# mLSTM values with tokens on the output's partitions, and scores and weights handled by pairs of heads

## The chip, the cores and the metric

The kernel runs on one core of one Trainium2 chip. The metric is the time of one execution on the device, in microseconds (us). Before the change three runs took 670.98, 671.68 and 671.97 us, a median of 671.68.

## What is computed

Four layers follow one another on a hidden state of 4 sequences of 256 tokens with 256 channels: attention with rotary parts, a gated feed-forward layer, an mLSTM block with its own feed-forward layer, and a feed-forward layer with int8 weights. Each ends in a layer norm of input plus output. The change lies in the mLSTM, of which this is the core (8 heads, 16 channels for queries and keys, 32 for values):

```python
Dmat = Fcum[..., :, None] - Fcum[..., None, :] + i_pre[..., None, :]
Dmat = jnp.where(causal, Dmat, -jnp.inf)
m = jnp.max(Dmat, axis=-1, keepdims=True)
Smat = jnp.exp(Dmat - m)
qk = jnp.einsum('bhsd,bhtd->bhst', q, k) / jnp.sqrt(jnp.float32(dqk))
C = qk * Smat
n = jnp.maximum(jnp.abs(jnp.sum(C, axis=-1, keepdims=True)), jnp.exp(-m))
h = jnp.einsum('bhst,bhtd->bhsd', C / n, v)
```

A root-mean-square norm per head, a sigmoid gate and the output projection follow.

## The kernel before, in words

Every engine has its own hand-written program (`@block.tensor`, `scalar`, `vector`, `gpsimd`, `sync`), and they meet by counting semaphores alone. Whatever stands behind a waiting instruction on its engine waits too. The order in each program is fixed by the loops `for c in range(B)` (4 sequences, called chunks here) and `for pair in range(PAIRS)` (4 pairs of heads), so there are 16 steps of one pair. This is the heads stage. Ahead of it stand the projections (L1482 to L1484), behind it the block's feed-forward layer (`ffn_pe` with kind 1, L1229 to L1269), into whose steps the rest of the head work of the last chunks is hooked (`finish_heads`).

One pair goes through five pieces of work before the change:

- **scores** (TensorE, L1548 and L1549): for each head, keys stand as the stationary operand (32 rows, 128 columns), queries stream: 256 columns, then 128, each in two parts of an fp32r split. A head has a PSUM bank of its own, UG0 or UG1, and may begin once the DVE has weighed the head two before it (`c_ready`).
- **decay** (ScalarE, L1720 and L1721): the exponential of the decay rows of one head, 256 and 128 columns, into one of four buffers.
- **weigh** (DVE, L1907): scores from PSUM times decay, 384 columns, for one head, into one of four weight buffers. The left 256 columns are key tile 0 against all 256 queries, the last 128 are key tile 1 against query tile 1.
- **values** (TensorE, L1563, L1565, L1567): the values `V1` of a head (128 tokens by 32 channels and a column of ones) stand as the stationary operand, 33 columns; the weights stream, 128 columns at a time. The output has channels on its partitions. The two heads of a pair use different halves of the array's columns (output partitions 0 to 32 and 64 to 96 of bank UG2 or UG3). These are fp32 matmuls, each of which is two instructions (two LDWEIGHTS and two MATMULs) in the trace.
- **take_pair** (ScalarE, L1729) copies that output into `gt`, and **back** (TensorE, L1576) transposes it, two transposes per pair, into the bank pair `OUTS`, with tokens on the partitions. After four pairs `take` (ScalarE, L1736) copies `OUTS` to `hraw`, and `squares`, `head_sums` (DVE, L1918 to L1925), `head_scales` (GpSimd, L2072 to L2083), `norm_b` (DVE, L1934, L1939), `heads_T` (TensorE, L1588), `hoT` and `project_out` (TensorE, L1482 again, output `X`) follow, some of them one or two chunks later.

TensorE also runs `keep_busy` (L1605), matmuls with no result that anybody reads: four after the first scores, one each in the steps (2, 0), (2, 1) and (3, 0) (chunk, pair). The DVE also adds the causal mask to the decay rows (`mask_rows`, L1898).

Of the kernel before, what the change touches and what calls it, by code (L numbers as in the profile page):

```python
# [21 lines left out]
P = 128  # L22
# [943 lines left out]
def layers(nc, keep, wl_d, wg_d, bg_d, cols_d, mask_d, wm_d, w8_d, sdown_d, out_d):  # L966
# [5 lines left out]
    with keep["both"], ExitStack() as ctx:  # L972
# [9 lines left out]
        def halves(a):  # L982
# [47 lines left out]

        A = [a[:, :].rearrange("p (h n) -> p h n", h=HM) for a in (stage, stage1)]

        decay_buf = [ga[:, 0, :], ga[:, 1, :], rows[:, 768:1152], rows[:, 1152:1536]]
        weight_buf = [gb[:, 0, :], gb[:, 1, :], rows[:, 0:384], rows[:, 384:768]]
        og_v = x1[:, :, :].rearrange("p (c t) d -> p c t d", c=B)
        scr_m = nc.dram_tensor("scr_m", (B, 32, S + P), F32).ap()

        UG = [pb(f"UG{i}") for i in range(4)]
        OUTS = pb("OUTS", (P, 2, 512))
        TB, X = keep["TB"], keep["X"]  # L1040

# [5 lines left out]
            st_ready e_ready c_ready pv_ready vt_ready back_ready taken abs_ready nn_ready n2_ready n2_squared sq_ready msq_ready hv_ready  # L1047
# [429 lines left out]
        def _(pe):  # L1477
# [61 lines left out]
            def scores(c, h):  # L1539

                r, n = slice(32 * (h % 4), 32 * (h % 4) + 32), (h // 4) * S
                if h == 0:
                    pe.wait_ge(s_["qk_split"], 2 * B if c == 0 else 2 * (c + 1))
                if c or h >= 2:
                    pe.wait_ge(s_["c_ready"], HM * c + h - 1)
                bank = UG[h % 2]
                for keys, q, out in ((n, slice(n, n + S), bank[:, 0:S]), (n + P, slice(n + P, n + S), bank[:, S:S + P])):
                    pe.matmul(out, stack(c, 1)[r, keys:keys + P], stack(c, 0)[r, q], start=True, stop=False)  # L1548
                    last = pe.matmul(out, stack(c, 2)[r, keys:keys + P], stack(c, 0)[r, q], start=False, stop=True)  # L1549
                last.then_inc(s_["st_ready"], 1)  # L1550

            def values(c, pair):

                two = (2 * pair, 2 * pair + 1)
                pe.wait_ge(s_["c_ready"], HM * c + 2 * pair + 2)
                if c == 0 and pair == 0:
                    pe.wait_ge(s_["og_ready"], TT * B)
                if c or pair >= 2:
                    pe.wait_ge(s_["vt_ready"], HM // 2 * c + pair - 1)
                w = [weight_buf[(HM * c + h) % 4] for h in two]  # L1560
                out = [UG[2 + pair % 2][i * 64:i * 64 + DH + 1, 0:S] for i in range(2)]
                for i, h in enumerate(two):
                    pe.matmul(out[i][:, 0:P], V1[:, c, 0, h, :], w[i][:, 0:P], start=True, stop=True)  # L1563
                for i, h in enumerate(two):
                    pe.matmul(out[i][:, P:S], V1[:, c, 0, h, :], w[i][:, P:S], start=True, stop=False)  # L1565
                for i, h in enumerate(two):
                    pe.matmul(out[i][:, P:S], V1[:, c, 1, h, :], w[i][:, S:S + P], start=False,  # L1567
                              stop=True).then_inc(s_["pv_ready"], 1)

            def back(c, pair):  # L1570

                pe.wait_ge(s_["vt_ready"], HM // 2 * c + pair + 1)
                if c and pair == 0:
                    pe.wait_ge(s_["taken"], c)
                for t in range(TT):
                    last = pe.transpose(OUTS[:, t, pair * P:pair * P + PAIR], gt[0:PAIR, pair % 2, t * P:(t + 1) * P],  # L1576
                                        ident[0:PAIR, 0:PAIR])
                last.then_inc(s_["back_ready"], 1)

            def heads_T(c):  # L1580
                pe.wait_ge(s_["ho_ready"], c + 1)
# [25 lines left out]
            def heads(c):  # L1607
                if c == 0:
                    scores(0, 0)
                    scores(0, 1)  # L1610
                    keep_busy(4)
                for pair in range(PAIRS):
                    if pair + 1 < PAIRS:
                        scores(c, 2 * pair + 2)
                        scores(c, 2 * pair + 3)
                    elif c + 1 < B:
                        scores(c + 1, 0)
                        scores(c + 1, 1)
                    if pair == 2 and c >= 2:
                        project_out(c - 2)  # L1620
                    if (c, pair) in ((2, 0), (2, 1), (3, 0)):
                        keep_busy(1)
                    values(c, pair)
                    if pair:
                        back(c, pair - 1)
                    elif c:
                        back(c - 1, PAIRS - 1)
                    if pair == 0 and c >= 2:
                        heads_T(c - 2)
                    if pair == 1 and c >= 3:  # L1630
                        pe_T(pe, 2, c - 3)
# [13 lines left out]
                heads(c)  # L1645

            def finish_heads(k, c, ht):
                if ht == 0:
                    back(3, PAIRS - 1)
# [22 lines left out]
        def _(act):  # L1672
# [41 lines left out]
            def decay(c, h):  # L1714
                if h % 2 == 0:
                    act.wait_ge(s_["masked_rows"], HM // 2 * c + h // 2 + 1)
                if c or h >= 4:
                    act.wait_ge(s_["c_ready"], HM * c + h - 3)
# [5 lines left out]
            def take_pair(c, pair):  # L1724

                act.wait_ge(s_["pv_ready"], HM * c + 2 * pair + 2)
                if c or pair >= 2:
                    act.wait_ge(s_["back_ready"], HM // 2 * c + pair - 1)
                act.activation(gt[0:PAIR, pair % 2, :], UG[2 + pair % 2][0:PAIR, 0:S], ACT.Copy).then_inc(s_["vt_ready"], 1)  # L1729
# [61 lines left out]
            decay(0, 3)  # L1791
            for c in range(B):
                for pair in range(PAIRS):
                    if pair:
                        take_pair(c, pair - 1)
                    elif c:
                        take_pair(c - 1, PAIRS - 1)
                    if pair == 1 and c:
# [12 lines left out]
            take_pair(3, PAIRS - 1)  # L1811

            def finish_heads(k, c, ht):
                if ht == 0:
                    take(3)
# [23 lines left out]
        def _(dve):  # L1839
# [60 lines left out]
            def weigh(c, h):  # L1900

                dve.wait_ge(s_["st_ready"], HM * c + h + 1)
                dve.wait_ge(s_["e_ready"], HM * c + h + 1)
                u = HM * c + h
                if u >= 4:
                    dve.wait_ge(s_["pv_ready"], u - 3)
                dve.scalar_tensor_tensor(weight_buf[u % 4], UG[h % 2][:, 0:384], 1.0 / math.sqrt(DQ), decay_buf[u % 4],  # L1907
                                         ALU.mult, ALU.mult).then_inc(s_["c_ready"], 1)

            def head_sums(c):  # L1910

# [59 lines left out]
            take_v(3, 1)  # L1971
            for c in range(B):
                for pair in range(PAIRS):
                    weigh(c, 2 * pair)
                    weigh(c, 2 * pair + 1)
# [245 lines left out]
```

## Time and profile before

| | |
|---|---|
| median of three runs | 671.68 us |
| the profiled execution's own time | 671.22 us |
| its span | 669.4 us |
| TensorE matmul busy | 656.9 us, 98% |
| TensorE weight load busy | 632.3 us, 94% |
| DVE, ScalarE, GpSimd busy | 439.2, 410.9, 246.3 us |
| heads stage | 502.4 to 539.7 us of the span |

Times in the rows are microseconds from the start of the span. A matmul that is written as 128*33 128x128 has 128 rows and 33 columns of stationary operand and streams 128 columns. PE is the stream of matmuls, PEld the weight loads, which run beside it; the end of a matmul is modelled and lies some time behind the moment at which its last column has entered, so it is the distance between starts or ends that tells what one of a series costs. In a timeline, neighbours of one kind are merged into one row with a count.

### The profile page before, as it was taken

The page shows a single profiled execution, that of the slowest core. Times are in us where ns is not written, and L with a number is a line of the kernel's source. Part 1 is how long each engine was busy: PE and PEld are TensorE (multiplying, and loading weights), DVE is VectorE, ACT ScalarE, POOL GpSimd, SP SyncE. Part 2 cuts the span into 40 slices and gives each one's busy share as a digit, 9 for nine tenths or more (in the row PEclk, how much of TensorE's full clock was granted, in tenths as well). Part 3 has the DMA queues.
Part 4 walks back from the last instruction along what each step waited for, and adds up shares of the span by engine and source line. Part 5 has one row for each costly group of instructions (what it writes and reads, how often), then busy time and mean ns, then how long its engine had stood idle before and what let it go on. Part 6 is the DMA issues. An engine that isn't in the chain of part 4 may idle for free. (4 is left out here: it accounts for less than half of the span.)

```text
span 669.4 us, 15275 instructions
## 1 busy us (share of the span) xinstructions
PE 656.9 (98%) x5297; PEld 632.3 (94%) x5297; DVE 439.2 (66%) x968; ACT 410.9 (61%) x1085; POOL 246.3 (37%) x279
## 2 busy tenths in 40 slices
PE   8999999999999999999999999999999999999995
PEld 8999999999999999999999899999997799999995
DVE  5566557656665765765675677556569986556877
ACT  5566667566776666766577773334689964333553
POOL 2731863034353133632329555112361462222011
PEclk9999999999999999999999999999999999999998
DMA  7174665435534445534363304100166100000010
GB/s 255 38 220 153 197 172 144 138 98 174 169 124 115 123 124 178 157 122 131 97 194 125 97 2 151 32 0 0 48 200 245 72 1 1 1 1 0 1 33 31
DMA packets 38172, 69.74 MB, mean 104 GB/s; under 512 B 3440, under 2 KB 22640, under 8 KB 37872
## 3 DMA queue, kind: packets, MB, share of 16 engines
q1 hardware_dynamic: 37696, 68.38, 33.6%
q10 hardware_dynamic: 432, 0.79, 0.4%
q8 instruction: 26, 0.43, 0.3%
q14 instruction: 18, 0.15, 0.1%
HBM read 52.18 MB, written 16.97 MB: 103 GB/s over the span
## 5 line engine op out<-in xcount | busy, mean ns | idle before, releaser
L312 PE MATMUL PJ<-xTh,WBh 128*128 128x256 f32 x364 | 106.7, 293 | 0.0
L314 PE MATMUL PJ<-xTh,WBl 128*128 128x256 f32 x364 | 103.0, 283 | 0.0
L313 PE MATMUL PJ<-xTl,WBh 128*128 128x256 f32 x364 | 102.8, 282 | 0.0
L851 POOL TENSOR_TENSOR stage<-stage 128x256 f32<-128x256 f32 x32 | 24.5, 766 | 162.8 <-DVE stage L718 162.8
L611 ACT ACTIVATE probs<-probs,rinv 128x256 f32<-128x256 f32 x128 | 58.4, 508 | 26.7 <-DVE rinv L734 26.7
L1229 PE MATMUL UG<-xTh,WBh 128*128 (+1 forms) x256 | 73.6, 288 | 0.3 <-PEq L54 0.3
L1232 PE MATMUL UG<-xTh,WBl 128*128 (+1 forms) x256 | 72.4, 283 | 0.0
L1230 PE MATMUL UG<-xTl,WBh 128*128 (+1 forms) x256 | 72.4, 283 | 0.0
L1301 ACT ACTIVATE ga<-UG 128x256 f32<-128x256 f32 x64 | 24.5, 383 | 75.5 <-PE UG L1232 75.5
L312 PEld LDWEIGHTS PJ<-xTh,WBh 128*128 128x128 f32 x364 | 69.6, 191 | 0.5
L313 PEld LDWEIGHTS PJ<-xTl,WBh 128*128 128x128 f32 x364 | 69.6, 191 | 0.0
L314 PEld LDWEIGHTS PJ<-xTh,WBl 128*128 128x128 f32 x364 | 69.4, 191 | 0.0
L723 DVE TENSOR_TENSOR QKl<-PJ,QKh 128x512 fp32r<-128x512 f32 x63 | 43.4, 690 | 37.2 <-ACT QKh L599 37.0
L1353 DVE TENSOR_TENSOR gb<-UG,ga 128x256 f32<-128x256 f32 x64 | 27.1, 423 | 43.8 <-ACT ga L1301 43.3
L866 POOL TENSOR_TENSOR WBl<-raw,WBh 128x512 fp32r<-128x512 f32 x32 | 40.9, 1301 | 29.2 <-ACT WBh L628 29.2
L1088 POOL TENSOR_SCALAR vare<-mv 128x2 f32<-128x2 f32 x13 | 2.9, 224 | 132.0 <-DVE mv L1081 132.0
L1229 PEld LDWEIGHTS UG<-xTh,WBh 128*128 128x128 f32 x256 | 49.0, 192 | 0.5 <-issue 0.5
L604 ACT ACTIVATE probs<-TB,nmax 128x256 f32<-128x256 f32 x64 | 29.8, 470 | 31.9 <-DVE nmax L730 30.4
L604 ACT ACTIVATE probs<-SC,nmax 128x256 f32<-128x256 f32 x64 | 29.8, 471 | 31.8 <-DVE nmax L730 31.8
L1230 PEld LDWEIGHTS UG<-xTl,WBh 128*128 128x128 f32 x256 | 49.1, 192 | 0.0
L1232 PEld LDWEIGHTS UG<-xTh,WBl 128*128 128x128 f32 x256 | 49.0, 191 | 0.0
L738 DVE TENSOR_TENSOR PTl<-PT,PTh 128x512 fp32r<-128x512 f32 x64 | 43.4, 678 | 5.4 <-ACT PTh L617 5.4
(326 smaller groups left out, 2364.1 us busy)
## 6 DMA issues: line engine op xcount, KB each, us to landing
K<-scr_k SPq DMA_DIRECT2D x60, 256.0 KB, 4.4
raw<-in_w_att SPq DMA_DIRECT2D x37, 256.0 KB, 4.8
Q<-scr_q SPq DMA_DIRECT2D x15, 512.0 KB, 7.5
stage<-scr_m SPq DMA_DIRECT2D x6, 768.0 KB, 4.4
scr_q<-rot_h SPq DMA_DIRECT2D x30, 128.0 KB
scr_q<-rot_l SPq DMA_DIRECT2D x30, 128.0 KB
scr_k<-rot_h SPq DMA_DIRECT2D x30, 128.0 KB
scr_k<-rot_l SPq DMA_DIRECT2D x30, 128.0 KB
```

Source lines behind the costliest of these rows:

```text
L312: pe.matmul(out, ah, bh, start=(i == 0), stop=False)
L313: pe.matmul(out, ah, bl, start=False, stop=False)
L314: last = pe.matmul(out, al, bh, start=False, stop=(i == n - 1))
L604: last = act.activation(probs[:, j % 2, t, :], SC[j % 2][:, t, :], ACT.Exp, scale=SCALE, bias=nmax[:, j % 2, t:t + 1], accum_out=rsum[:, j ...
L611: last = act.activation(probs[:, j % 2, t, :], probs[:, j % 2, t, :], ACT.Copy, scale=rinv[:, j % 2, t:t + 1])
L723: dve.tensor_tensor(part_dst(k, p, False), bank_of(k, p)[:, :], part_dst(k, p, True).bitcast(F32), ALU.subtract).then_inc(part_split, 1)
L738: dve.tensor_tensor(PTl[:, j % 2, :, :], PT[:, :, :], PTh[:, j % 2, :, :].bitcast(F32), ALU.subtract).then_inc(pT_split, 1)
L866: pool.tensor_tensor(weights(i, False), raw[:, i % RING, :], weights(i, True).bitcast(F32), ALU.subtract).then_inc(w_split, 1)
L1229: pe.matmul(out, wh, xh_v[:, t, c, :], start=(t == 0), stop=False)
L1230: last = pe.matmul(out, wh, xl_v[:, t, c, :], start=False, stop=(kind == 2 and t == KT - 1))
L1232: last = pe.matmul(out, w_up(kind, t, ht, which, False), xh_v[:, t, c, :], start=False, stop=(t == KT - 1))
L1353: dve.tensor_tensor(y, u, ga[:, ht % 2, 0:S], ALU.mult).then_inc(q["gated"], 1)
```

## The change

- `values` swaps its operands: the weights (128 by 128, fp32) stand in the array, one load for each instruction, and `V1` streams with 33 columns. The output has tokens on its partitions and goes straight into `OUTS`; `back`, `take_pair` and their semaphores `vt_ready` and `back_ready` are gone.
- The four banks UG0 to UG3 all hold scores, two for a pair, written two pairs ahead. The two heads' instructions alternate.
- `weigh` handles a pair in one DVE instruction over two banks, 768 columns; `c_ready` counts pairs.
- `take` is moved from step (c, 1) to step (c, 0) and waits for the values themselves (`pv_ready`); the values of a chunk's first pair wait for `taken` of the chunk before.
- `project_out` and `keep_busy` stand ahead of the scores of their step, not behind them. The second pair's first scores wait for `og_ready`, since UG2 and UG3 still hold the last projections.

```diff
@@ layers
-        decay_buf = [ga[:, 0, :], ga[:, 1, :], rows[:, 768:1152], rows[:, 1152:1536]]
-        weight_buf = [gb[:, 0, :], gb[:, 1, :], rows[:, 0:384], rows[:, 384:768]]
+        decay_pairs = [ga[:, :, :], rows[:, 768:1536].rearrange("p (h n) -> p h n", h=2)]
+        weight_pairs = [gb[:, :, :], rows[:, 0:768].rearrange("p (h n) -> p h n", h=2)]
...
-        UG = [pb(f"UG{i}") for i in range(4)]
+        UGS = pb("UGS", (P, 4, 512))
+        UG = [UGS[:, i, :] for i in range(4)]
@@ scores
+                two = (2 * pair, 2 * pair + 1)
...
+                if c == 0 and pair == 1:
                     pe.wait_ge(s_["og_ready"], TT * B)
                 if c or pair >= 2:
+                    pe.wait_ge(s_["c_ready"], PAIRS * c + pair - 1)
+                r = [slice(32 * (h % 4), 32 * (h % 4) + 32) for h in two]
+                bank = [UG[2 * (pair % 2) + i] for i in range(2)]
+                for keys, q, out in ((n, slice(n, n + S), slice(0, S)), (n + P, slice(n + P, n + S), slice(S, S + P))):
+                    for i in range(2):
+                        pe.matmul(bank[i][:, out], stack(c, 1)[r[i], keys:keys + P], stack(c, 0)[r[i], q],
+                                  start=True, stop=False)
+                    for i in range(2):
+                        last = pe.matmul(bank[i][:, out], stack(c, 2)[r[i], keys:keys + P], stack(c, 0)[r[i], q],
+                                         start=False, stop=True)
@@ values
-                out = [UG[2 + pair % 2][i * 64:i * 64 + DH + 1, 0:S] for i in range(2)]
-                for i, h in enumerate(two):
-                    pe.matmul(out[i][:, 0:P], V1[:, c, 0, h, :], w[i][:, 0:P], start=True, stop=True)
...
+                for h in (2 * pair, 2 * pair + 1):
+                    w = weight_buf[(HM * c + h) % 4]
+                    out = [heads_v[:, t, h, :] for t in range(TT)]
+                    pe.matmul(out[0], w[:, 0:P], V1[:, c, 0, h, :], start=True, stop=True)
+                    pe.matmul(out[1], w[:, P:S], V1[:, c, 0, h, :], start=True, stop=False)
+                    pe.matmul(out[1], w[:, S:S + P], V1[:, c, 1, h, :], start=False, stop=True)\
+                        .then_inc(s_["pv_ready"], 1)
@@ heads
-                    if pair + 1 < PAIRS:
-                        scores(c, 2 * pair + 2)
-                        scores(c, 2 * pair + 3)
...
                     if pair == 2 and c >= 2:
                         project_out(c - 2)
                     if (c, pair) in ((2, 0), (2, 1), (3, 0)):
                         keep_busy(1)
+                    if pair + 2 < PAIRS:
+                        scores(c, pair + 2)
+                    elif c + 1 < B:
+                        scores(c + 1, pair + 2 - PAIRS)
                     values(c, pair)
-                    if pair:
-                        back(c, pair - 1)
-                    elif c:
-                        back(c - 1, PAIRS - 1)
@@ take
-                act.wait_ge(s_["back_ready"], HM // 2 * (c + 1))
+                act.wait_ge(s_["pv_ready"], HM * (c + 1))
@@ weigh
+                u, at = HM * c + 2 * pair, pair % 2
+                dve.wait_ge(s_["st_ready"], u + 2)
+                dve.wait_ge(s_["e_ready"], u + 2)
                 if u >= 4:
+                    dve.wait_ge(s_["pv_ready"], u - 2)
+                dve.scalar_tensor_tensor(weight_pairs[at], UGS[:, 2 * at:2 * at + 2, 0:384], 1.0 / math.sqrt(DQ),
+                                         decay_pairs[at], ALU.mult, ALU.mult).then_inc(s_["c_ready"], 1)
```

## Rows read from the trace of the kernel before

**Rows 1.** Heads stage: length; PE, PEld, DVE, ACT, POOL busy; PE clock; DMA.
```profile
502.40:539.70 37.30, 36.30 (x395) 28.49 (x395) 34.59 (x72) 33.11 (x99) 13.69 (x15) 1.00 0.36 139
```

**Rows 2.** Waits within the heads stage: us in total, times, longest.
```profile
PE UG L1548 <- DVE rows L1907: 0.9, 3, 0.4
DVE gb L1907 <- PE UG L1549: 0.8, 3, 0.3
```

**Rows 3.** Timeline of PE, one step: start us, us, instruction.
```profile
508.00 0.39 PE L1548 MATMUL UG<-WI 32*128 32x256 f32 x2
...
508.61 0.41 PE L1563 MATMUL UG<-gb,V 128*33 128x128 f32 x4
...
509.08 0.39 PE L1567 MATMUL UG<-gb,V 128*33 128x128 f32 x4
509.39 0.39 PE L1576 MATMUL OUTS<-ident,gt 97*128 97x97 f32 x2
509.71 0.46 PE L1548 MATMUL UG<-WI 32*128 32x256 f32 x2
```

**Rows 4.** Timeline of PE, the scores of one head alone, then values.
```profile
505.84 0.38 PE L1548 MATMUL UG<-WI 32*128 32x256 f32 x1 [0.22 <-DVE rows L1907]
...
506.18 0.22 PE L1548 MATMUL UG<-WI 32*128 32x128 f32 x1
506.24 0.27 PE L1549 MATMUL UG<-WI 32*128 32x128 f32 x1
...
506.90 0.30 PE L1563 MATMUL UG<-rows,V 128*33 128x128 f32 x1
```

**Rows 5.** Groups of weight loads in the heads stage: busy us, mean ns of one.
```profile
L1548 PEld LDWEIGHTS UG<-WI 32*128 32x128 f32 x64 | 8.0, 182 | 3.7 <-issue 1.1 <-DVE rows L1907 1.1 <-DVE gb L1907 0.4
L1576 PEld LDWEIGHTS OUTS<-ident,gt 97*128 97x128 f32 x30 | 3.0, 140 | 3.0 <-issue 2.8 <-ACT gt L1729 0.2
L1563 PEld LDWEIGHTS UG<-gb,V 128*33 128x33 f32 x32 | 1.2, 109 | 1.0 <-issue 0.5
```

**Rows 6.** Timeline of PE and ACT, start of the heads stage.
```profile
502.95 0.39 ACT L1694 ACTIVATE x<-UG 128x256 f32<-128x256 f32 x1 [0.38 <-DVE V L1881]
...
503.00 1.20 PE L1605 MATMUL TB<-WLh 128*128 128x512 f32 x4
504.13 0.42 PE L1548 MATMUL UG<-WI 32*128 32x256 f32 x2
```

**Rows 7.** Timeline of PE, `project_out` (12 instructions), and four transposes from the chain.
```profile
525.78 0.39 PE L1482 MATMUL X<-WLh 128*128 128x256 f32 x1
...
527.20 0.28 PE L1484 MATMUL X<-WLh,WLl 128*128 128x256 f32 x1
...
553.30 0.44 PE X L1588 x4
```

**Rows 8.** Groups of ScalarE in the heads stage.
```profile
L1729 ACT ACTIVATE gt<-UG 97x256 f32<-97x256 f32 x15 | 5.6, 375 | 3.4 <-PE UG L1567 3.3
L1736 ACT ACTIVATE hraw<-OUTS 128x528 f32<-128x528 f32 x3 | 1.8, 606 | 0.0
```

**Rows 9.** Timeline of PE, end of the heads stage.
```profile
539.38 0.39 PE L1576 MATMUL OUTS<-ident,gt 97*128 97x97 f32 x2
539.55 0.36 PE L1229 MATMUL UG<-xTh,WBh 128*128 128x256 f32 x1
...
541.05 0.33 PE L1576 MATMUL OUTS<-ident,gt 97*128 97x97 f32 x2
```

**Rows 10.** Groups of DVE over the whole span, by form.
```profile
L1907 DVE SCALAR_TENSOR_TENSOR gb<-UG,ga 128x384 f32<-128x384 f32 x16 | 8.1, 549 | 0.8 <-PE UG L1549 0.8
L1851 DVE TENSOR_TENSOR WI<-stage,WI 128x896 fp32r<-128x896 f32 x1 | 1.1, 1082 | 0.0
```

**Rows 11.** End of the span, columns as in rows 1.
```profile
660.00:664.40 4.40, 2.69 (x18) 2.11 (x17) 3.54 (x11) 1.20 (x3) 0.00 (x0) 1.00 0.17 60
664.40:669.40 5.00, 0.00 (x0) 0.00 (x0) 1.99 (x6) 0.00 (x0) 1.89 (x4) 0.50 0.16 52
```

More of the change, by code:

```diff
@@ L1031, in layers @@
         A = [a[:, :].rearrange("p (h n) -> p h n", h=HM) for a in (stage, stage1)]
-        decay_buf = [ga[:, 0, :], ga[:, 1, :], rows[:, 768:1152], rows[:, 1152:1536]]
-        weight_buf = [gb[:, 0, :], gb[:, 1, :], rows[:, 0:384], rows[:, 384:768]]
+        decay_pairs = [ga[:, :, :], rows[:, 768:1536].rearrange("p (h n) -> p h n", h=2)]
+        weight_pairs = [gb[:, :, :], rows[:, 0:768].rearrange("p (h n) -> p h n", h=2)]
+        decay_buf = [pair[:, i, :] for pair in decay_pairs for i in range(2)]
+        weight_buf = [pair[:, i, :] for pair in weight_pairs for i in range(2)]
         og_v = x1[:, :, :].rearrange("p (c t) d -> p c t d", c=B)
         scr_m = nc.dram_tensor("scr_m", (B, 32, S + P), F32).ap()
-        UG = [pb(f"UG{i}") for i in range(4)]
+        UGS = pb("UGS", (P, 4, 512))
+        UG = [UGS[:, i, :] for i in range(4)]
         OUTS = pb("OUTS", (P, 2, 512))
@@ L1046, in layers @@
             chain_step m_ready nm_ready m_out masked_rows rows_ready gcol_ready enm_ready
-            st_ready e_ready c_ready pv_ready vt_ready back_ready taken abs_ready nn_ready n2_ready n2_squared sq_ready msq_ready hv_ready
+            st_ready e_ready c_ready pv_ready taken abs_ready nn_ready n2_ready n2_squared sq_ready msq_ready hv_ready
             hsc_ready hs_ready ho_ready hoT_ready hoT_hi hoT_split wo_ready x1_ready x1_mid""".split()
@@ L1537, in rows_T, with scores @@
                 last.then_inc(s_["rows_ready"], 1)
-            def scores(c, h):
-                r, n = slice(32 * (h % 4), 32 * (h % 4) + 32), (h // 4) * S
-                if h == 0:
+            def scores(c, pair):
+                two = (2 * pair, 2 * pair + 1)
+                n = (pair // 2) * S
+                if pair == 0:
                     pe.wait_ge(s_["qk_split"], 2 * B if c == 0 else 2 * (c + 1))
[L1544 to L1556, printed above, removed]
+                if c == 0 and pair == 1:
                     pe.wait_ge(s_["og_ready"], TT * B)
                 if c or pair >= 2:
-                    pe.wait_ge(s_["vt_ready"], HM // 2 * c + pair - 1)
-                w = [weight_buf[(HM * c + h) % 4] for h in two]
-                out = [UG[2 + pair % 2][i * 64:i * 64 + DH + 1, 0:S] for i in range(2)]
-                for i, h in enumerate(two):
-                    pe.matmul(out[i][:, 0:P], V1[:, c, 0, h, :], w[i][:, 0:P], start=True, stop=True)
[L1564 to L1568, printed above, removed]
@@ L1570, in back @@
-            def back(c, pair):
-                pe.wait_ge(s_["vt_ready"], HM // 2 * c + pair + 1)
+                    pe.wait_ge(s_["c_ready"], PAIRS * c + pair - 1)
[8 more added lines that the diff above has]
+                                         start=False, stop=True)
+                        if keys != n:
+                            last.then_inc(s_["st_ready"], 1)
@@ L1573, in back, with values @@
+            def values(c, pair):
+                pe.wait_ge(s_["c_ready"], PAIRS * c + pair + 1)
                 if c and pair == 0:
                     pe.wait_ge(s_["taken"], c)
[L1575 to L1578, printed above, removed]
+                for h in (2 * pair, 2 * pair + 1):
[5 more added lines that the diff above has]
+                        .then_inc(s_["pv_ready"], 1)
@@ L1612, in heads @@
                 for pair in range(PAIRS):
-                    if pair + 1 < PAIRS:
-                        scores(c, 2 * pair + 2)
-                        scores(c, 2 * pair + 3)
-                    elif c + 1 < B:
-                        scores(c + 1, 0)
-                        scores(c + 1, 1)
                     if pair == 2 and c >= 2:
@@ L1647, in finish_heads @@
             def finish_heads(k, c, ht):
-                if ht == 0:
-                    back(3, PAIRS - 1)
                 if ht == 1:
@@ L1717, in decay @@
                 if c or h >= 4:
-                    act.wait_ge(s_["c_ready"], HM * c + h - 3)
+                    act.wait_ge(s_["c_ready"], PAIRS * c + h // 2 - 1)
                 e, a, at = decay_buf[(HM * c + h) % 4], A[c % 2], 32 * c + h
@@ L1722, in decay @@
                                bias=gcol[:, 1, at:at + 1]).then_inc(s_["e_ready"], 1)
[L1724 to L1729, printed above, removed]
             def take(c):
-                act.wait_ge(s_["back_ready"], HM // 2 * (c + 1))
+                act.wait_ge(s_["pv_ready"], HM * (c + 1))
                 if c:
@@ L1793, in _ @@
                 for pair in range(PAIRS):
[L1794 to L1798, printed above, removed]
+                    if pair == 0 and c:
                         take(c - 1)
@@ L1898, in mask_rows, with weigh @@
                 dve.tensor_tensor(a, a, m, ALU.add).then_inc(s_["masked_rows"], 1)
[L1900 to L1904, printed above, removed]
+            def weigh(c, pair):
+                u, at = HM * c + 2 * pair, pair % 2
+                dve.wait_ge(s_["st_ready"], u + 2)
+                dve.wait_ge(s_["e_ready"], u + 2)
                 if u >= 4:
-                    dve.wait_ge(s_["pv_ready"], u - 3)
-                dve.scalar_tensor_tensor(weight_buf[u % 4], UG[h % 2][:, 0:384], 1.0 / math.sqrt(DQ), decay_buf[u % 4],
-                                         ALU.mult, ALU.mult).then_inc(s_["c_ready"], 1)
+                    dve.wait_ge(s_["pv_ready"], u - 2)
+                dve.scalar_tensor_tensor(weight_pairs[at], UGS[:, 2 * at:2 * at + 2, 0:384], 1.0 / math.sqrt(DQ),
+                                         decay_pairs[at], ALU.mult, ALU.mult).then_inc(s_["c_ready"], 1)
             def head_sums(c):
@@ L1973, in _ @@
                 for pair in range(PAIRS):
-                    weigh(c, 2 * pair)
-                    weigh(c, 2 * pair + 1)
+                    weigh(c, pair)
                     if c == 0 and pair == 0:
```

1 line of the change is left out of this document (removed).

## The prediction

> **What bounds the kernel now.** I began with the busy time by stretch, for the heads stage alone, since the change touches nothing else. TensorE is busy for 36.30 of its 37.30 us, the DVE for 34.59, ScalarE for 33.11, at the full 2.4 GHz (clock 1.00) [rows 1]. Three engines are nearly full, so the waits come next: TensorE waited 0.9 us for a weigh, the DVE 0.8 us for scores [rows 2]. These two hand the lead to each other. Behind the stage TensorE streams without a gap [rows 9] up to where it ends [rows 11], so a microsecond won or lost here reaches the end whole.
>
> A busy TensorE may be a TensorE at work on something cheap, so I read a single step from its timeline [rows 3]: scores of a pair 0.61 us (508.00 to 508.61), values 0.78 (to 509.39), back 0.32 (to 509.71), together 1.71. Sixteen of these are 27.4 of the 37.3 us; the rest is keep_busy, project_out, the transposes and about 3 us of stalls, some of them the scores of a single head that had to go alone [rows 4].
>
> Values take 0.78 us for 12 instructions because the two heads run side by side in the two halves of the array: start to start from L1563 to L1567, four instructions deep in each half, is 0.47 us, less 0.03 for the first load 0.11 for each two instructions [rows 3]. Six times 0.11, the 0.03, and some 0.10 in which the array turns from one shape of tile to the next, make 0.78.
>
> **What a weight load costs.** This decides the case, since the new values load 128 columns for every 33 that they stream. Three rows price a load. The first instruction of a burst waits for its own load: scores 0.38 where a later one with as many columns has 0.28, so 0.10 for 128 columns of fp32r [rows 4]; values 0.30 where later ones have 0.27, so 0.03 for 33 columns [rows 4]. Where little streams, loads set the pace: the last two matmuls of a head stream 128 columns and end at 506.40 and 506.51, 0.11 apart, though they start 0.06 apart [rows 4]. The mean of a load, 109 ns for 33 columns, 182 ns for 128, 140 ns for the 128 of a transpose, says the same: 0.07 more for 95 more columns, and the transposes, alone, half of that [rows 5]. No row has an fp32 load of 128 columns that isn't a transpose's. I take 0.113 us for an instruction of the new values (the pace where little streams), since 33 and 128 columns lie on one line of 0.8 ns a column. The bounds are 0.06 (a transpose's load, 0.055, and a little) and 0.14 (0.113 and the 0.028 of streaming, if the two don't overlap).
>
> The Trainium skill (TensorE: Matmul & The Clock Gate, section LDWEIGHTS) gives a load as columns over 1.2, thus 107 ns for 128 columns and 27 for 33. The rows agree but for the transposes. By it alone the sum below would be an estimated 1.2 us smaller, and still a loss.
>
> **The change on TensorE.** A step after: scores 0.61 as before (they already run side by side when both heads are free). Values 12 x 0.113 = 1.36, 0.03 of last streaming, 0.10 to turn the array: 1.49. Back is gone. Together 2.10 instead of 1.71, 0.39 more for each of 16 steps.
>
> I walk through the stage with it.
> - Scores of pair 0 start at 502.4. Those of pair 1 now wait for the last gate projection, taken from UG at 503.34 [rows 6]; they go at 503.4 and end at 504.0.
> - Four keep_busy with their turns, 1.13 [rows 6]: 505.1, where it was 504.1. The DVE is not held up, its masks and first weigh lie here.
> - Fourteen steps of scores and values: 29.4.
> - Three keep_busy of one at about 0.23 (1.13 less a turn and a first load, over four): 0.7. Two project_out: 12 instructions from 525.78 to 527.32 [rows 7], 1.5 each, 3.0. Three sets of transposes at 0.44 and a load [rows 7]: 1.4.
> - Values of the last two pairs, without scores: 2.7.
> - The new wait for `taken`: at the turn of a chunk the values stand behind `take`, 0.61 [rows 8], and the pick-up on both sides, about 0.9 in all from the last streamed column. Scores (0.61 and a turn), with a keep_busy in two of three chunks, cover 0.7 to 0.9 of it. Behind the waiting values on TensorE stand all later scores, but those are two pairs ahead. I put down 0.3 for three turns.
>
> That ends at 542.6. Before, the last transposes of the stage were through at 539.6 [rows 9]: 3.0 later. Behind the stage the back of the last pair is gone, two transposes at 541.05 and a new load, 0.2 [rows 9]. **Sum: 2.8 us slower.**
>
> **The change elsewhere.** ScalarE loses 16 copies of 0.375 [rows 8], about 4.5 us by their pace; it wasn't the bound, so this is worth nothing in itself. The DVE's weigh goes from two of 549 to one. A line through 384 columns of this operation and 896 of a tensor_tensor (549 and 1082 ns) gives 949 for 768 [rows 10], against 1.02 for two that overlap: 0.07 a pair, 1.1 us in all. Bounds: 0.95 to 1.10, since no row reads two banks in this form. It is worth nothing while TensorE leads: the DVE needs about 33.5 us where TensorE needs 40. Its work is uneven: weigh p+1 waits for the values of p-1, so the DVE can be one step ahead, and this lead of about 2 us is what hides norm_b, dve_xs and hoT in chunks 2 and 3. I take it as enough and put down nothing; if it isn't, project_out and the transposes wait for the DVE, up to 1 us. The chain over GpSimd to norm_b has the same two steps as before, each now longer. No DMA is issued or moved; nothing is added for SP and GpSimd.
>
> The Trainium skill (TensorEngine Tiling (Array Packing), When to Use Tiling) advises, for a right-hand side of 64 columns or less, to swap the operands and tile by columns. That is the form before, and here the rows agree that its two heads run together. The change goes the other way: by the rule it is a loss, by my step 0.71 us a pair in values, of which back returns 0.32.
>
> **Rivals.**
> - **A cheap load (faster).** If fp32 loads of 128 columns cost what a transpose's cost, 0.06 for an instruction, values take 0.85 and a step 1.46. TensorE is then through at 532 and the DVE leads: its last weigh, 537.65 before, comes 1.1 (its gain) and 1.1 (its waits for scores) earlier, and the values end at 536.2, 3.4 early; 0.2 more is won behind, and I allow 0.5 for hooked transposes that then meet a DVE without a lead. 3.1 faster: 668.6. For it: the transposes' 140 ns. Against: 33 and 128 columns lie on one line. The point where it decides is 0.098 for an instruction (2.8 over 192 instructions below 0.113).
> - **Loads and streams take turns.** 0.14 for an instruction, 192 x 0.028 = 5.4 more: 679.9. Against: in rows 4 loads run under the stream.
> - **The clock falls.** The array streams less in the new values (0.34 of 1.49 us). Were the loads at 1.2 GHz, 192 x 0.107 = 20 us more, half of it if it fell for half of the stage: 10 to 20 more than the main case, 684 to 695. Against: between 660 and 664.4 TensorE was busy for 2.69 of 4.4 us at 1.00, and fell to 0.50 only once it had stopped [rows 11].
> - **A wash.** A load at 0.10 and no other stall: within 1.3 us of before.
>
> **How the numbers follow.** The profiled execution took 671.22 us, 0.46 less than the median of 671.68. With 2.8 it gives 674.0, and against the median 674.5. What this kernel's measurement can tell from no change is 0.2%, 1.34 us. Chances: the main case 0.70 (at times it comes out under 1.34, say 0.04 of it), cheap load 0.16, turns 0.05, clock 0.04, wash 0.05. Slower by over 0.2% is then 0.75, the same 0.09, faster 0.16. The range leaves out the cheap load and the clock: 671.0 to 680.0.
>
> **What would show it.** In the profile after, PEld of the values with 128*128 x192, ends 0.11 apart; a mean of such a load near 185 ns (140 would be the rival). A stage from 502.4 to about 542.5. Steps of 2.1 us. The DVE waiting for PE (L1907 behind the values), TensorE hardly for the DVE. Weigh near 0.95. No L1576, no L1729. PE clock 1.00 in the stage. I am wrong if the values' instructions come 0.06 apart, if TensorE waits over 1 us for weighs, or if the stage ends before 539.6.

## The result, and the profile after

The changed kernel takes 696.3 us (median of 4 runs, 694.96 to 700.35) where the kernel before takes 671.58. The ratio is 1.0379, 95% interval 1.0335 to 1.0423. The forecast was 674.5 in a range of 671.0 to 680.0: the sign was right, the size was not. The profiled execution took 694.96 us, its span is 693.1.

The length of each stretch, from the first and last matmul of each in the two timelines, says where it went: the heads stage is 62.40 us long (500.96 to 563.36) where it was 37.16 (502.38 to 539.54), 25.2 more. What lies behind it is 0.1 shorter. What lies ahead of it is the same code in both kernels; the stage began 1.4 us earlier in this execution, and among all the profiles of this study its first scores start anywhere from 500.9 to 502.8. So stages are compared by their length below.

The first view is the busy time of three stretches of the heads stage after the change. The columns are those of [rows 1].

```profile
500.96:509.50 8.54, 8.21 (x79) 7.24 (x78) 7.07 (x10) 6.85 (x19) 0.00 (x0) 1.00 0.87 314
509.50:560.70 51.20, 51.20 (x264) 47.65 (x264) 26.12 (x46) 22.29 (x63) 13.62 (x15) 0.50 0.13 48
560.70:563.30 2.60, 2.60 (x26) 2.60 (x24) 2.05 (x4) 1.55 (x5) 0.41 (x2) 0.99 0.03 6
```

For 51.2 us the granted clock is 0.50, that is 1.2 GHz in place of 2.4. TensorE is busy for all of them, and in the 8.54 us before the fall for 8.21: it didn't fall because TensorE stood idle. The DVE and ScalarE are busy for about half: now TensorE alone is the bound. The page shows the same at a glance, beside a line of nines before:

```profile
PE   8999999999999999999999999999999999999996
DVE  6566556765775576656655766565665466655877
PEclk9999999999999999999999999999975589999999
```

The PE line tells nothing of it: a matmul at half the clock is busy for longer and looks as full as before.

The timeline of PE shows how the new values run at either level. These are the first of the 16 steps, at 2.4 GHz, the starts of the two after it, and one step at 1.2 GHz:

```profile
503.71 0.38 PE L1556 MATMUL UGS<-WI 32*128 32x256 f32 x2
...
504.31 0.41 PE L1572 MATMUL OUTS<-V,gb 128*128 128x33 f32 x2
504.55 0.39 PE L1573 MATMUL OUTS<-V,gb 128*128 128x33 f32 x2
504.78 0.39 PE L1574 MATMUL OUTS<-V,gb 128*128 128x33 f32 x2
505.00 0.39 PE L1572 MATMUL OUTS<-V,gb 128*128 128x33 f32 x2
505.22 0.39 PE L1573 MATMUL OUTS<-V,gb 128*128 128x33 f32 x2
505.45 0.39 PE L1574 MATMUL OUTS<-V,gb 128*128 128x33 f32 x2
505.77 0.38 PE L1556 MATMUL UGS<-WI 32*128 32x256 f32 x2
...
507.83 0.38 PE L1556 MATMUL UGS<-WI 32*128 32x256 f32 x2
...
544.72 0.58 PE L1556 MATMUL UGS<-WI 32*128 32x256 f32 x2
...
545.76 0.64 PE L1572 MATMUL OUTS<-V,rows 128*128 128x33 f32 x2
546.21 0.62 PE L1573 MATMUL OUTS<-V,rows 128*128 128x33 f32 x2
546.63 0.61 PE L1574 MATMUL OUTS<-V,rows 128*128 128x33 f32 x2
```

From 504.55 to 505.45 lie eight instructions in 0.90 us, 0.112 each, for 33 streamed columns: the load sets the pace, as the forecast had it (0.113). A step lasts 2.06 (503.71 to 505.77, to 507.83), forecast 2.10, where it was 1.71 [rows 3]. At the lower clock an instruction costs 0.21 (546.21 to 546.63, two of them), and a step's scores 1.04 (544.72 to 545.76) where they cost 0.60. The weight loads of the three steps at the higher clock, as groups with their mean:

```profile
L1559 PEld LDWEIGHTS UGS<-WI 32*128 32x128 f32 x12 | 1.1, 184 | 0.0
...
L1574 PEld LDWEIGHTS OUTS<-V,gb 128*128 128x128 f32 x6 | 0.9, 192 | 0.0
```

The fp32 load of 128 columns has 192 ns, beside 184 for fp32r and 140 for a transpose [rows 5]; the rival of the cheap load is out.

On the other engines, the groups of the DVE's weigh in the stage, with the time that it was idle before them:

```profile
L1883 DVE SCALAR_TENSOR_TENSOR gb<-UGS,ga 128x768 f32<-128x768 f32 x8 | 7.7, 958 | 13.6 <-PE OUTS L1574 13.4 <-PE UGS L1559 0.2
L1883 DVE SCALAR_TENSOR_TENSOR rows<-UGS,rows 128x768 f32<-128x768 f32 x8 | 7.6, 956 | 8.4 <-PE OUTS L1574 7.3 <-ACT ga L1710 1.0
```

A pair costs 957 ns in one instruction, forecast 949 from [rows 10]. The DVE waits 20.7 us for the values (13.4 and 7.3). Before, it waited 1.1 for scores: 0.8 for one of its two pairs of buffers [rows 2] and 0.3 for the other.

So two theories remained. Theory A: the clock fell because the new values stream too few columns beside their loads. Theory B: it fell because of the 128-column fp32 loads, or of the way the array turns between tile shapes.

### The profile page after: what moved, and what is told of

The parts are those of the page before. It is cut to its first block and busy times, and to the rows that moved or that the text cites. A ratio compares the mean times of both kernels' runs of the same rounds, so it can differ in the third digit from the quotient of the medians.

```text
span 693.1 us, 15134 instructions
## 1 busy us (share of the span) xinstructions
PE 681.5 (98%) x5265; PEld 660.7 (95%) x5265; DVE 437.4 (63%) x952; ACT 407.0 (59%) x1069; POOL 245.6 (35%) x279
## 5 line engine op out<-in xcount | busy, mean ns | idle before, releaser
L1232 PE MATMUL UGS<-xTh,WBh 128*128 (+1 forms) x256 | 73.5, 287 | 0.3 <-PEq L54 0.3
L1235 PE MATMUL UGS<-xTh,WBl 128*128 (+1 forms) x256 | 72.4, 283 | 0.0
L1233 PE MATMUL UGS<-xTl,WBh 128*128 (+1 forms) x256 | 72.4, 283 | 0.0
L1304 ACT ACTIVATE ga<-UGS 128x256 f32<-128x256 f32 x64 | 24.5, 383 | 76.5 <-PE UGS L1235 76.5
L1356 DVE TENSOR_TENSOR gb<-UGS,ga 128x256 f32<-128x256 f32 x64 | 27.1, 423 | 44.4 <-ACT ga L1304 43.9
L1232 PEld LDWEIGHTS UGS<-xTh,WBh 128*128 128x128 f32 x256 | 49.1, 192 | 0.5 <-issue 0.5
L1233 PEld LDWEIGHTS UGS<-xTl,WBh 128*128 128x128 f32 x256 | 49.1, 192 | 0.0
L1235 PEld LDWEIGHTS UGS<-xTh,WBl 128*128 128x128 f32 x256 | 49.0, 192 | 0.0
```

Of the source, the lines that this page charges most:

```text
L1232: pe.matmul(out, wh, xh_v[:, t, c, :], start=(t == 0), stop=False)
L1233: last = pe.matmul(out, wh, xl_v[:, t, c, :], start=False, stop=(kind == 2 and t == KT - 1))
L1235: last = pe.matmul(out, w_up(kind, t, ht, which, False), xh_v[:, t, c, :], start=False, stop=(t == KT - 1))
L1356: dve.tensor_tensor(y, u, ga[:, ht % 2, 0:S], ALU.mult).then_inc(q["gated"], 1)
```

## The experiments

**One column count.** In `wide64` and `wide128` the values stream more of `V1`; the output goes into columns of `OUTS` that nobody reads or that the next head overwrites.

```diff
 # wide128; wide64 has 64 in place of m
-                    out = [heads_v[:, t, h, :] for t in range(TT)]
-                    pe.matmul(out[0], w[:, 0:P], V1[:, c, 0, h, :], start=True, stop=True)
+                    m = 128 if h < HM - 1 else 64
+                    out = [OUTS[:, t, 64 * h:64 * h + m] for t in range(TT)]
+                    v = [V1t[:, (HM * (TT * c + t) + h) * (DH + 1):(HM * (TT * c + t) + h) * (DH + 1) + m] for t in range(TT)]
+                    pe.matmul(out[0], w[:, 0:P], v[0], start=True, stop=True)
 ... (the other two likewise; V1t is V1 as one row, with some zeros behind its end)
```

> The changed kernel, with one thing altered: the values stream 64 columns in place of 33 (the 31 more are a neighbour's values and land in columns of OUTS that nobody reads). Instructions, loads and waits stay the same. Theory A, the clock fell because the new values stream too few columns beside their loads: the clock stays at 1.00 in the heads stage, a values instruction still costs 0.112 us (the stream of 64 fp32 columns, 0.053, hides under the load of 0.107), and the kernel takes 673 to 675 us, the 2 to 3 us of the dearer loads and no more. Theory B, the clock fell because of the loads themselves or of the change of tile shape, whatever is streamed: clock at 0.50 for some 50 us again, 694 to 700 us. Between them, 680 to 690, if it falls for a shorter stretch.

Measured: 693.76 us, ratio 1.0344 (1.0331 to 1.0357). The clock fell at 508.9, came back at 543.0 for 6.8 us, and fell again until 560.1:

```profile
508.90:543.00 34.10, 34.10 (x174) 31.59 (x176) 17.90 (x30) 16.14 (x44) 7.88 (x8) 0.50 0.21 78
```

What theory A said of 64 columns (clock 1.00, 673 to 675) failed, and the time lies just under theory B's 694 to 700. The 6.8 us only hint that the amount has an effect.

> As wide64, with 128 streamed columns in the values of seven heads of eight (64 in the eighth): the stream of 128 fp32 columns takes 0.107 us, as long as the load beside it, so instructions, loads, waits and, within a few ns, the pace stay those of the changed kernel. In wide64 the clock fell as before but came back for 6.8 us in between, so the amount streamed seems to count and 64 was too few. Theory A (what is streamed decides): now as dense as the old form, clock 1.00 in the stage, 673 to 675.5 us. Theory B (128-column fp32 loads or the turn of the tile shape decide): the clock is at 0.50 for 40 to 50 us again, 693 to 700 us.

Measured: 674.81 us, ratio 1.0068 (1.0049 to 1.0086). The busy time of its heads stage, columns as in [rows 1]:

```profile
501.20:543.10 41.90, 40.24 (x366) 36.20 (x365) 34.05 (x59) 30.17 (x86) 14.40 (x16) 1.00 0.32 124
```

The clock stayed at 1.00 with the same loads, the same turns of the array and the same instructions. Theory B is out, and what is left of the loss is 3.7 us by the medians. It isn't the chip either: `values_only`, below, ran on the same chip, and there the clock fell. One step of its timeline, and the turn of a chunk ahead of it:

```profile
512.76 0.38 PE L1558 MATMUL UGS<-WI 32*128 32x256 f32 x2
...
513.16 0.27 PE L1561 MATMUL UGS<-WI 32*128 32x128 f32 x2
513.62 0.46 PE L1576 MATMUL OUTS<-V,gb 128*128 128x128 f32 x2 [0.19 <-ACT hraw L1722]
...
515.13 0.39 PE L1558 MATMUL UGS<-WI 32*128 32x256 f32 x2
...
517.27 0.38 PE L1558 MATMUL UGS<-WI 32*128 32x256 f32 x2
```

The step is 2.14 (515.13 to 517.27), 0.08 more than with 33 columns, 1.3 us over 16 steps. All of it lies at the start of the values, where the second group of two instructions comes 0.32 behind the first instead of 0.24. At 513.62 the values wait for `take`: the start comes 0.46 behind the last score, where it is 0.2 elsewhere. The waits of PE in this stage:

```profile
PE OUTS L1576 <- ACT hraw L1722: 1.3, 3, 0.8
PE UGS L1558 <- ACT x L1687: 0.3, 1, 0.3
```

Three chunks turned for 1.3 us; I had put down 0.3. Most of it isn't the length of `take` (0.61). Here are the three of them on ScalarE:

```profile
512.87 0.61 ACT L1722 ACTIVATE hraw<-OUTS 128x528 f32<-128x528 f32 x1 [1.58 <-PE OUTS L1578]
...
522.49 0.61 ACT L1722 ACTIVATE hraw<-OUTS 128x528 f32<-128x528 f32 x1 [2.23 <-DVE ho L1920]
...
533.77 0.61 ACT L1722 ACTIVATE hraw<-OUTS 128x528 f32<-128x528 f32 x1 [1.98 <-DVE ho L1920]
```

The first starts when the values end, and TensorE then waits 0.19. The other two start only once the DVE has finished `ho`, the normed and gated heads of the chunk before (`take` waits for it too, since it overwrites `hraw`, from which they are made), and there TensorE waits 0.78 and 0.36, 1.14 of the 1.3.

**Less streamed, same loads as before.** The next two runs start from `hybrid`, which keeps the scores, the pair weigh and the order of the change and goes back to the old values:

```diff
+                out = [[UG[2 * (pair % 2) + t][i * 64:i * 64 + DH + 1, 384:512] for t in range(TT)] for i in range(2)]
+                for i, h in enumerate(two):
+                    pe.matmul(out[i][0], V1[:, c, 0, h, :], w[i][:, 0:P], start=True, stop=True)
 ... (the other two likewise; take_pair, back and take as before)
 # weigh
-                    dve.wait_ge(s_["pv_ready"], u - 2)
+                    dve.wait_ge(s_["vt_ready"], u // 2 - 1)
```

> The other parts of the change without the new values: scores by pairs in four banks two pairs ahead, a pair weighed in one instruction, and the order of the changed kernel, but values, take_pair and back as before (channels on the partitions, 33-column loads, output in the free 128 columns of the score banks; a weigh also waits for take_pair two pairs before). Theory A: the whole loss comes from the values; here the step on TensorE is 1.71 us as before and the waits between DVE and TensorE go, 668 to 671 us at clock 1.00. Rival: the scores two ahead or the pair weigh bring a wait of their own (a weigh that begins only when both heads' scores and take_pair are done): 672 to 676.

Measured: 669.46 us, ratio 0.9982 (0.9973 to 0.9991), 0.2% less than the kernel before. Its heads stage is 36.31 us long:

```profile
501.20:537.50 36.30, 33.75 (x394) 26.08 (x394) 33.97 (x56) 32.70 (x97) 13.14 (x15) 1.00 0.38 140
```

Now TensorE has slack and the DVE, at 33.97 of 36.30, is the bound. So the other parts of the change bring no loss by themselves; it takes the new values.

```diff
 # hybrid64, the same in all three matmuls
-                    pe.matmul(out[i][0], V1[:, c, 0, h, :], w[i][:, 0:P], start=True, stop=True)
+                    pe.matmul(out[i][0][:, 0:64], V1[:, c, 0, h, :], w[i][:, 0:64], start=True, stop=True)
```

> The hybrid with only 64 of each 128 columns streamed in the old-form values (the second half of the tokens' values is left out). Loads, tile shapes and instruction counts stay those of the hybrid, which held 1.00. Theory A (what is streamed decides): the clock falls in the stage for 10 to 50 us, 674 to 690 us. Theory B (loads of 128 fp32 columns are needed): clock 1.00, at or below the hybrid's 669.5 us.

Measured: 674.55 us, ratio 1.0048 (1.0028 to 1.0068), at less work on TensorE than the hybrid's 669.46. The busy time of two stretches:

```profile
504.00:511.90 7.90, 6.92 (x98) 5.19 (x96) 7.71 (x12) 7.78 (x24) 0.00 (x0) 1.00 0.74 273
511.90:542.60 30.70, 30.68 (x251) 25.05 (x252) 24.03 (x41) 24.00 (x70) 11.38 (x15) 0.50 0.22 79
```

Half of the values' columns taken away, and the clock fell for 30.7 us, without any 128-column fp32 load in the values. It did so in all seven executions, whose mean clocks are 0.974 to 0.986 where the hybrid's twelve are 0.996 to 0.998. That is theory A from the other side. With less to do, TensorE also stood idle more here before the fall, busy 6.92 of 7.90 us where in the hybrid it is 7.75, so by itself this run can't tell fewer columns from more idling. The changed kernel can: there the clock fell without idling.

**Filler matmuls.** Does it matter where the columns come from? Three kernels add `keep_busy` to the changed kernel.

```diff
-                    if (c, pair) in ((2, 0), (2, 1), (3, 0)):
+                    if 4 * c + pair < 14:
                         keep_busy(1)   # busy_each; 3 in busy_three, 8 in busy_eight
```

> The changed kernel with one keep_busy matmul (512 columns, nobody reads it) in each of the first 14 steps, where it had three. Theory A (too little streaming): the clock stays at 1.00, and the time is that of wide64 plus 11 matmuls at 0.23 us, 2.5 us: 676 to 678. Theory B (loads or tile shapes): the clock falls again, 697 to 705.

Measured: 700.12 us, ratio 1.0467 (1.0434 to 1.05). The clock fell at 509.6 all the same, came back at 547.1 for 3.4 us and fell again until 564.2. The time is the one written down for theory B: after wide128 it says that one filler a step was too few, and theory A's number was wrong.

> The changed kernel with three keep_busy matmuls in each of the first 14 steps. One a step (busy_each) didn't hold the clock, 128 streamed columns in the values (wide128) did. If the amount streamed is what counts, wherever it comes from: clock 1.00 for most of the stage, and the time is 674.8 less about 1 (33 columns in place of 128) plus 39 matmuls at 0.22 us, 8.6: 681 to 684 us. If filler matmuls don't hold it as the values' own columns do: over 700.

Measured: 710.32 us, ratio 1.0601 (1.0554 to 1.0649). A miss: of the two cases I had written down it is the worse one.

```profile
504.50:516.50 12.00, 12.00 (x102) 10.02 (x102) 7.44 (x11) 6.21 (x17) 0.00 (x0) 1.00 0.53 196
516.50:577.80 61.30, 61.30 (x279) 53.51 (x280) 26.21 (x47) 21.95 (x61) 15.84 (x18) 0.50 0.07 26
```

The fall came 7 us later than in the changed kernel, at 516.5, and then lasted for the rest of the stage, which the fillers had made longer, and 3.6 us beyond it. After this a rival stood within theory A: that the thin stretches of values themselves do it, and no filler between them can help.

> The changed kernel with eight keep_busy matmuls in each of the first 14 steps, 1.7 us of dense streaming after each 1.4 us of values. With three the clock fell 7 us later than with none and stayed down. Theory T (the total streamed counts, wherever it comes from, and three a step were too few): clock 1.00 in the stage, 674 plus 109 matmuls at 0.215 us, 23: 695 to 699 us. Theory S (the stretches of values themselves decide, fillers between them can't hold it): the clock falls and stays at 0.50, over 725 us.

Measured: 699.41 us (2 runs), ratio 1.0424 (1.0393 to 1.0454), 0.4 above the range for theory T. The whole heads stage:

```profile
502.80:567.80 65.00, 64.67 (x473) 54.69 (x473) 35.17 (x59) 30.38 (x86) 13.87 (x16) 1.00 0.21 78
```

The clock held through the whole stage, although each step has the same 1.4 us of 33-column values. So the columns of fillers count too; one or three matmuls a step were too few. As a remedy it is worthless: the fillers cost what the clock gives back.

**The parts alone.** `values_only` is the kernel before with the new values and nothing else, `values_only128` the same with 128 streamed columns, `weigh_pair` the kernel before with the pair weighed at once.

```diff
 # values_only, on the kernel before
-                out = [UG[2 + pair % 2][i * 64:i * 64 + DH + 1, 0:S] for i in range(2)]
+                    out = [heads_v[:, t, h, :] for t in range(TT)]
 ... (values as in the change; take_pair and back gone; scores and weigh per head stay)
 # weigh_pair, on the kernel before
-                dve.scalar_tensor_tensor(weight_buf[u % 4], UG[h % 2][:, 0:384], 1.0 / math.sqrt(DQ), decay_buf[u % 4],
+                dve.scalar_tensor_tensor(weight_pairs[at], UGS[:, 0:2, 0:384], 1.0 / math.sqrt(DQ), decay_pairs[at],
```

> The kernel before with the new values alone (tokens on the output's partitions, take_pair and back gone, take moved); scores per head one ahead in two banks and a weigh per head as before. Both theories: the clock falls, 693 to 700 us, since the values are what changed the pace. Rival: the two-ahead scores have a share in the fall (they remove the waits for the DVE, in which the array rests, so this one should then be worse, over 700) or the fall needs them (then 674 to 677 at 1.00).

Measured: 699.91 us, ratio 1.0418 (1.0388 to 1.0448). The clock was low for 64.9 us from 507.1 on, and TensorE was never idle in them. The scores two ahead are not needed for the fall. Whether they have a share in its length stays open: 699.91 lies at the rival's bound of 700.

> The kernel before with the new values alone, 128 columns streamed as in wide128 so that the clock should hold. It prices the values by themselves. If the loss of wide128 (3.7 us on the median) is the values' alone and the other parts are worth their 1.2 us here too: clock 1.00, 675 to 677 us. If the two-ahead scores are worth more beside dear values than in the hybrid (per-head scores that wait for the DVE now lengthen a step of 2.1 us): 678 to 682. If the other parts only pay beside the old values: 673.5 to 675.

Measured: 678.67 us, ratio 1.0118 (1.0103 to 1.0133), with one dip of 3.4 us in its profile. Less wide128's 1.0068 this makes the other parts worth 0.5%, 3.4 us, beside the dear values, and 0.18% beside the old ones. Not all of the 3.4 is work saved: the dip alone cost some 1.7 (an estimate, half its length), and all four executions have mean clocks of 0.992 to 0.995, where five of wide128's six have 0.996 to 0.998.

> The kernel before with the pair weighed in one instruction over the two score banks and nothing else: scores of the next pair wait until both heads are weighed and then run side by side. If the one instruction (0.95 for 1.02 us) and the scores side by side win: 669.5 to 671. If the scores' longer wait costs, since with two banks the DVE now waits for every pair's scores, 0.6 us each but for what other DVE work hides: 672 to 677.

Measured: 671.19 us, ratio 1.0008 (0.9997 to 1.0018), between the two forecasts. The one instruction alone brings no gain that can be measured: with two score banks the engines wait for each other as before, the DVE more than it did. Its profile has a dip of the clock too, 3.4 us from 519.2, so a part of its time is clock. Its waits, to be read beside [rows 2]:

```profile
DVE gb L1910 <- PE UGS L1552: 2.1, 6, 1.0
...
PEld UGS L1551 <- DVE gb L1910: 1.7, 7, 0.4
PE UGS L1551 <- DVE rows L1910: 1.3, 2, 0.7
```

**How near the old stage stood.** `before_no_kb` is the kernel before without its three single keep_busy.

```diff
-                    if (c, pair) in ((2, 0), (2, 1), (3, 0)):
-                        keep_busy(1)
```

> The kernel before without its three single keep_busy matmuls (the four at the start stay). If the clock keeps its level in the old heads stage without them: 670.2 to 671.6, three matmuls with their turns at up to 0.43 us each less, part of which falls into waits for the DVE. If the old stage too hung on them: the clock falls, 680 to 700.

Measured: 670.74 us, ratio 1.0004 (0.999 to 1.0018), a median like the one before, but single runs of 672.69, 674.5 and 675.15 among eleven. The profiled one is of these:

```profile
518.20:531.80 13.60, 13.60 (x93) 10.64 (x94) 9.44 (x21) 8.58 (x24) 5.43 (x5) 0.50 0.24 89
```

Those three executions have mean clocks of 0.986 to 0.988, the other eight 0.996 to 0.998. The kernel before, in the 78 executions that were measured beside these experiments, never went under 0.993, and reached that in five (672.46 to 674.22 us). So the old stage already stood near the fall, and without the three matmuls it fell for longer in 3 of 11.

**Towards a better version.** `hybrid_late` puts project_out and keep_busy behind the scores of their step again, `hybrid_busy` adds keep_busy in (0, 3), (1, 1) and (1, 3).

```diff
 # hybrid_late
-                    (project_out and keep_busy here)
                     if pair + 2 < PAIRS:
                         scores(c, pair + 2)
 ...
+                    (project_out and keep_busy here)
 # hybrid_busy
-                    if (c, pair) in ((2, 0), (2, 1), (3, 0)):
+                    if (c, pair) in ((0, 3), (1, 1), (1, 3), (2, 0), (2, 1), (3, 0)):
```

> The hybrid with project_out and keep_busy behind the scores of their step, as in the kernel before. In the hybrid's profile project_out waited some 2.6 us in two places for the DVE's hoT, with the scores standing behind it. If those waits sit on the path: 668 to 669.2 us, up to 1 us less than the hybrid's 669.5. If they only move to the next wait for a weigh, since the DVE is the bound there (33.97 of 36.30 us busy): 669.2 to 670.

Measured: 670.35 us, ratio 0.9985 (0.9974 to 0.9996) beside a kernel before of 671.34 on this chip: no better than the hybrid. Its profile has a dip of the clock of 3.4 us. The expectation's 2.6 us counts the same two waits twice, once for the matmuls (0.48 and 0.61, so 1.1) and once for their loads (0.67 and 0.84, so 1.5).

> The hybrid with a keep_busy more in the steps (0, 3), (1, 1) and (1, 3), since a profile of a near relative (hybrid_late) had a dip of the clock of 3.4 us at 519, in chunk 1. TensorE has slack in the hybrid. If such dips cost the hybrid something in its mean: 668.5 to 669.3. If the three matmuls stand on the path: 669.6 to 670.3.

Measured: 670.21 us, ratio 0.9979 (0.9969 to 0.9988) beside 671.48; 669.06 to 671.05 over eleven runs. By the ratio it is as good as the hybrid, and a cost of the three more matmuls doesn't show; the median lies in the range for matmuls on the path, 0.75 above the hybrid's, but the kernel before was as much slower here (671.48) than beside the hybrid (670.75).

## Why the prediction was right in its sum and wrong in its time

The step that failed is the clock. Every term of the sum was taken at 1.00, and the rival "The clock falls" got a chance of 0.04 and no part of the range. Measured, the clock was 0.50 for 51.2 us of the stage, which costs some 21 us. The main case, all its terms at a clock of 1.00, is what wide128 shows.

- **A load of 128 fp32 columns at 0.113 for an instruction**: 0.112. The two rows that gave it, a first instruction's extra 0.10 and ends 0.11 apart [rows 4], were the right ones; the transposes' mean [rows 5] was no guide.
- **A step of 2.10**: 2.06 with 33 columns.
- **The stage 3.0 us longer at the full clock**: it was never seen with 33 columns. wide128 is 41.47 long, 4.3 more than before; less the 1.3 of its wider stream that is 3.0, an estimate from two profiles. That it meets the forecast's 3.0 is in part luck: the wait for `taken` was 1.0 too small, the step 0.04 too large in 14 of them, 0.6, and the values of the last two pairs went in at 2.7 where two times the step's own 1.49 is 3.0. Put right, these three give 3.7; what takes 0.7 off again isn't shown.
- **The DVE's lead is enough, put down as nothing**: this is where the wait for `taken` went wrong. It was priced by the length of `take`, 0.61, but in two of three turns `take` itself waited for the DVE's `ho`. The prediction had such a wait for the DVE, up to 1 us, but for project_out and the transposes.
- **The first scores of pair 1 wait for the gate projection**: in the profile after, 0.33 of idle before the scores at 501.96, as walked through.
- **Sum 2.8 slower at 1.00**: wide128 is 3.7 slower by the medians (4.6 by the ratio, interval 3.3 to 5.8), with the 1.3 in it.
- **The clock's price**: the stage of the changed kernel is 62.40 long, wide128's 41.47, so 20.9 us, some 22 without the wider stream. "20 more, half of it if it fell for half" was about right, 684 to 695 for a median of 696.3, but two errors met in it. I had counted the loads of all 192 instructions; some 136 of them lie in the low stretch, and at 0.10 more for each they make some 13 us (an estimate from these rows). The other 8 or 9 are scores, transposes, keep_busy and project_out, which are slower at 1.2 GHz as well and which I had left out.
- **Its chance** was the mistake. I noted that the new values stream 0.34 of 1.49 us, and then argued against the fall with a stretch at the end of the span in which TensorE was busy for 2.69 of 4.4 us [rows 11]. Busy time includes waiting for a load, and after the change it is 51.20 of 51.20 at half the clock. It says nothing of how much is streamed. What the profile did hold and I passed over is in the kernel: keep_busy exists, in three chosen steps. That these matmuls were there isn't a proof, but taking them away is a question to the trace of before that I couldn't put; before_no_kb puts it, and shows a stage near the fall (3 of 11 executions).
- The two pages of the Trainium skill named in the prediction agree with this case: loads at columns over 1.2 (TensorE: Matmul & The Clock Gate, LDWEIGHTS), with 0.112 measured for 0.107 at the granted clock of 1.00, though 0.21 at 0.50; and the swap with column tiling for small right-hand sides (TensorEngine Tiling (Array Packing), When to Use Tiling), since going the other way lost even at the full clock (wide128, 3.7 us).

What stays open: what the chip measures exactly when it grants the clock. The runs show the direction (128 streamed columns in the values held it, and so did eight fillers a step), not the amount. In all of them the columns streamed and the results written to PSUM rise and fall together, so which of the two counts isn't shown. Nor was the wait for `taken` taken away by itself, which needs a second `OUTS`.

## What to carry to other kernels

Before swapping the operands of a matmul, count for each instruction the columns loaded and the columns streamed: here 128 loaded for 33 streamed made the pace the load's, 0.11 us, and two heads that ran side by side in the array no longer could. Then ask what the swap does to the streaming of a whole stage, since where it thins out the clock may fall, and then all of TensorE's work in the stage, not the changed part alone, costs nearly double (here 0.21 for 0.112 and 1.04 for 0.60); a matmul busy line near 100% can't warn of it. When a change has several parts, run the hybrid: here the parts around the values were worth 0.2% once the values were left as they were.

## What the runs showed that I had not expected

- The granted clock fell 8.5 us behind the stage's start (500.96 to 509.5), and stayed low for 51.2 us although TensorE was never idle, through two project_out as well; in values_only it came back only in the dense feed-forward layer, at 572.0.
- Streaming 128 columns in place of 33, results that nobody reads, made the kernel 21.5 us faster by the medians (696.3 to 674.81).
- Halving the streamed columns of the hybrid's values made the kernel 5 us slower (669.46 to 674.55; 4.4 by the ratios).
- No number of fillers paid, and the one that held the clock isn't the best: 700.12 with one a step, 710.32 with three, 699.41 with eight, beside 696.3. By the ratios one and three a step are slower than the changed kernel beyond the intervals; eight isn't.
- A wait that is put down to `take` on ScalarE was at bottom one for the DVE, two engines away from TensorE.
